# A decoder layer on one core: the cross-attention keys are split a stage earlier, and two orders of work are rewritten

## The reference, cut to what matters

```python
x = x + attention(layernorm(x), Wq, Wk, Wv, Wo)       # causal; 32 heads of 16 in 8 groups; batch 4, 512 tokens, width 512
x = x + cross(layernorm(x), ctx, ctx)                 # 8 heads; per batch q, k, v are (8, 64, 512) views of the 512 x 512 array
x = x + ffn(layernorm(x), w_gate, w_up, w_down)       # 2048 wide, quantised: weights to -1, 0, 1, activations to 8 bits
# cross, for each of the 4 x 8 heads (m, n over 512 columns, d over 64 rows):
qk = einsum('bdm,bdn->bmn', qh, kh) / 8
ret = einsum('bmn,bcn->bcm', softmax(qk, axis=-1), vh)
# quantised weight: clip(round(w / scale), -1, 1), scale = mean(|w|) + 1e-5
```

## Time and profile before

| | us |
|---|---|
| median of 3 runs (range) | 791.97 (790.47 to 792.49) |
| the profiled execution's own time | 791.34 |
| its span in the trace | 789.5 |
| busy: PE, DVE, ACT, POOL | 758.5, 637.8, 491.1, 423.1 |
| projections, to the first full step | about 0 to 98 |
| self-attention, to the barrier | about 98 to 373.9 |
| attention output | 373.9 to about 435 |
| cross-attention | about 435 to 595 |
| feed-forward | about 595 to 789 |

### The profile page before, as it was taken

How to read it: one execution, slowest core, us unless ns; L and a number is a source line. 1 busy time by engine, 2 the same in 40 slices (tenths; PEclk the granted TensorE clock), 3 DMA queues, 4 the chain that set the end, 5 groups by cost and what they waited for, 6 DMA issues and landing times.

```text
span 789.5 us, 15365 instructions
## 1 busy us (share of the span) xinstructions
PE 758.5 (96%) x4832; PEld 420.6 (53%) x4886; DVE 637.8 (81%) x1905; ACT 491.1 (62%) x844; POOL 423.1 (54%) x459
## 2 busy tenths in 40 slices
PE   8999999999999999998999899999998999999998
PEld 6777544444444444443777555555543455455543
DVE  7676888889888889881589878888977899888883
ACT  4665567667766776676355555555556576567564
POOL 5554489999999700000234367777886444423331
PEclk9999999999999999999899999999999999999999
DMA  8898674444544311200486434444420011000001
GB/s 289 301 385 282 210 186 136 122 132 133 139 128 130 96 54 52 61 18 3 146 284 236 162 108 136 134 136 135 121 70 18 11 42 41 28 15 27 28 26 42
DMA packets 65888, 94.79 MB, mean 120 GB/s; under 512 B 27184, under 2 KB 38576, under 8 KB 64272
## 3 DMA queue, kind: packets, MB, share of 16 engines
q1 hardware_dynamic: 61344, 80.77, 32.5%
q0 software_dynamic: 3952, 12.98, 5.8%
q10 hardware_dynamic: 512, 0.07, 0.1%
HBM read 72.88 MB, written 20.51 MB: 118 GB/s over the span
## 4 chain that ended last, share of the span: by engine, by line
PE 40%; DVE 5%; issue 3%; ACT 2%; POOL 1%; SPq 0%; DMA 0%; ACTq 0%; DVEq 0%; POOLq 0%
PE r_p L1698 12%; PE r_p L1633 7%; PE r_pn L1646 7%; PE r_p L1728 3%; PE r_pn L1728 3%; PE r_p L1605 3%; PE r_p L1661 2%; PE r_p L1712 2%; DVE r_stats L1384 1%; DVE tok L1403 1%; PE r_p L1587 1%; DVE r_xl L1397 1%; ACT r_xn L1235 1%; DVE r_mx L1416 0%; DVE r_h L1500 0%
## 5 line engine op out<-in xcount | busy, mean ns | idle before, releaser
L787 ACT ACTIVATE b_probs<-ab_j 128x512 f32<-128x512 f32 (+1 forms) x352 | 176.7, 560 | 25.5 <-PE ab_j L852 14.6
L148 DVE CUSTOM_DVE_ANT_0 b_junk<-ab_t,mask_qk 128x128 bf16<-128x128 f32 (+2 forms) x243 | 108.7, 485 | 27.0 <-PE ab_t L128 26.7
L852 PE MATMUL ab_j<-qs,ks 98*128 98x512 bf16 (+1 forms) x352 | 121.8, 361 | 2.9 <-DMA qs<-mrow 1.1
L1277 ACT ACTIVATE r_probs<-r_p 128x512 f32<-128x512 f32 x128 | 69.5, 599 | 65.2 <-PE r_p L1633 63.8
L148 DVE CUSTOM_DVE_ANT_0 b_junk<-ab_e,mask_qk 128x256 bf16<-128x256 f32 (+2 forms) x237 | 103.6, 482 | 0.3 <-issue 0.2
L1416 DVE TENSOR_REDUCE r_mx<-r_p 128x1 f32<-128x512 f32 x128 | 82.4, 675 | 22.1 <-PE r_p L1605 21.2
L1175 POOL TENSOR_TENSOR r_halves<-r_probs 128x1024 f32<-128x1024 f32 x32 | 76.6, 2395 | 34.8 <-DVE r_total L1446 24.9
L1327 ACT ACTIVATE r_silu<-r_p,r_cg 128x512 f32<-128x512 f32 x64 | 44.2, 691 | 53.0 <-PE r_p L1698 51.7
L870 PE MATMUL ab_pv<-b_probs,v 128*32 128x512 f32 (+3 forms) x1024 | 75.6, 436 | 0.0
L1202 POOL TENSOR_SCALAR r_h<-r_h,r_fh 128x1024 f32<-128x1024 f32 x32 | 38.0, 1199 | 64.8 <-DVE r_fh L1546 64.8
L128 PE MATMUL ab_e<-ks,qs 96*128 96x128 bf16 (+3 forms) x269 | 64.0, 300 | 5.3 <-DVE mx L148 0.7
(11 more groups left out here) (177 smaller groups left out, 1761.3 us busy)
## 6 DMA issues: line engine op xcount, KB each, us to landing
qs<-q_parts SPq DMA_DIRECT2D x32, 192.0 KB, 3.3
q_parts<-a_parts SPq DMA_DIRECT2D x15, 384.0 KB, 6.1
a_wst<-in_w_gate SPq DMA_DIRECT2D x4, 1024.0 KB, 7.7
a_wst<-in_w_up SPq DMA_DIRECT2D x4, 1024.0 KB, 9.9
a_wst<-in_w_down SPq DMA_DIRECT2D x4, 1024.0 KB, 8.3
qs<-q_parts SPq DMA_DIRECT2D x32, 128.0 KB, 3.2
b_wst<-in_w_gate POOLq DMA_DIRECT2D x16, 256.0 KB, 3.8
b_wst<-in_w_up POOLq DMA_DIRECT2D x16, 256.0 KB, 3.3
```

The costliest lines, as they stand in the source:

```text
L148: best = nc.vector.tensor_tensor_reduce(out=junk[:, 2 * (st.use[i, k] % slots) + n, 0:w], in0=bank[:, c:c + w], in1=keep["mask_qk"][:, SEQ ...
L787: nc.scalar.activation(pblock(j % 2, kb)[:, j0:j0 + nj, c:c + w], p2[(NE * j + n) % BANKS2][:, 0:nj * w].rearrange("p (j c) -> p j c", j=n ...
L852: last = nc.tensor.matmul(bank, ks[0:STACK + 2, s, kb * P:(kb + 1) * P], qs[0:STACK + 2, s, j0:j0 + nj, kb * P + c:kb * P + c + w], start= ...
L1277: nc.scalar.activation(probs[:, 2 * (p % 2) + a, blk, :], p2_bank("s", j, n)[:], ACT.Exp, scale=SCALE).then_inc(p2_used, 1)
```

## The change

Three things change.

1. The step of self-attention has another order on PE, on DVE (through `Steps.order`) and on ACT, where `osb` is kept after the ninth exponential instead of the fifth.
2. The split of the keys moves from cross-attention into self-attention's steps 21 to 36, one pair per step: GpSimd loads the raw rows after it has quantised all weights, ACT makes the high part at the end of its step, GpSimd subtracts and stores both parts to DRAM, and cross-attention's SP loads both. The pairs of steps 34, 35 and 36 follow on ACT straight after its last `osb`. GpSimd waits for the last stores before the barrier. With it the second of the three quantising instructions gets a second operation (subtract, min), and the third becomes max, min.
3. `sum_probs` works once for four heads, with weights of 32 columns; the totals have 8 slots, sums and reciprocals go by four heads, and the final multiplication of a pair moves from body 13 to body 17 behind its first. `D_LAST` grows by four, so twelve feed bodies lie beside `attend_context` instead of eight.

```diff
-        self.order = [0, 1, self.OUT, 2, self.TURN] + list(range(3, self.nu))
+        self.order = [0, 1, 2, self.TURN, 3, 4, 5, 6, 7, self.OUT, 8, 9]
...
+    KPAIRS, KEYS_FROM = BATCH * XHEADS // 2, LAST - BATCH * XHEADS // 2
+    key_raw = wst[:, 0:2, :]
+    key_h = nc.alloc_sbuf_tensor_at("b_key_h", [P, 2, DIM], F32R, offset=keep["wst_at"] + 2 * 4 * DIM)
+    key_l = nc.alloc_sbuf_tensor_at("b_key_l", [P, 2, DIM], F32R, offset=keep["wst_at"] + 4 * 4 * DIM)
+    PARTS = KD * FF // PART
+    key_in, key_high, key_low, key_out = wst_in[0:2], wq2, wq1, m.sems("key_out", 2)
+    LOADED, QUANTISED = 16 * PARTS, 3 * PARTS
...
-            nc.gpsimd.tensor_scalar(out, raw, MAGIC, None, ALU.subtract).then_inc(wq2, 1)
+            nc.gpsimd.tensor_scalar(out, raw, MAGIC, 1.0, ALU.subtract, ALU.min).then_inc(wq2, 1)
             pool.wait_ge(wq2, t + 1)
-            nc.gpsimd.tensor_scalar(out, out, 1.0, -1.0, ALU.min, ALU.max)
+            nc.gpsimd.tensor_scalar(out, out, -1.0, 1.0, ALU.max, ALU.min)
...
+        def load_keys(p):
+            if p >= KPAIRS:
+                return
+            if due(p - 1):
+                pool.wait_ge(key_low, QUANTISED + p - 1)
+            pool.dma_start(key_raw[:, p % 2, :], io["ctx"][P * p:P * (p + 1), :]).then_inc(key_in[p % 2], 16)
+
+        def split_keys(p):
+            pool.wait_ge(key_high, QUANTISED + p + 1)
+            if due(32 * (p // 2)):
+                pool.wait_ge(key_out[p % 2], 32 * (p // 2))
+            nc.gpsimd.tensor_tensor(key_l[:, p % 2, :], key_raw[:, p % 2, :], key_h[:, p % 2, :].bitcast(F32), ALU.subtract).then_inc(key_low, 1)
+            pool.wait_ge(key_low, QUANTISED + p + 1)
+            for name, tile in (("kh", key_h), ("kl", key_l)):
+                pool.dma_start(scr[name][P * p:P * (p + 1), :], tile[:, p % 2, :].bitcast(F32)).then_inc(key_out[p % 2], 16)
+
+        pool.wait_ge(wq2, QUANTISED)
+        load_keys(0)
+        load_keys(1)
+        for p in range(KPAIRS):
+            split_keys(p)
+            load_keys(p + 2)
+        for s in range(2):
+            pool.wait_ge(key_out[s], 32 * (KPAIRS // 2))
...
-            for n in range(5):
+            for n in range(9):
...
-            for n in range(5, NE):
+            for n in range(9, NE):
                 exponential(n)
+            p = i - KEYS_FROM
+            if 0 <= p < KPAIRS:
+                act.wait_ge(key_in[p % 2], LOADED + 16 * (p // 2 + 1))
+                if due(32 * (p // 2)):
+                    act.wait_ge(key_out[p % 2], 32 * (p // 2))
+                nc.scalar.activation(key_h[:, p % 2, :], key_raw[:, p % 2, :], ACT.Copy).then_inc(key_high, 1)
...
-            F(0); S(0); F(1); S(1)
+            F(0); F(1); S(0); F(2)
+            W(0); W(1); W(2); W(3)
+            turn_maxima(nc, pe, st, keep, i)
+            S(1); F(3); S(2); S(3); F(4); F(5); S(4); S(5); F(6); F(7); S(6); S(7)
             turn_outputs()
-            F(2); S(2)
-            turn_maxima(nc, pe, st, keep, i)
-            F(3); S(3)
-            F(4); S(4)
-            W(0); W(1); W(2); W(3)
-            F(5); S(5); F(6); S(6); F(7); S(7); F(8); S(8); F(9); S(9); S(10)
+            S(8); F(8); S(9); F(9); S(10)
...
+            def load_keys(p):
+                if p >= 2:
+                    sp.wait_ge(k_in[p % 2], 16 * (p // 2))
+                if due(STEP * 2 * (p - UNROLL + 1)):
+                    sp.wait_ge(scores, STEP * 2 * (p - UNROLL + 1))
+                sp.dma_start(kh[:, p % UNROLL, :].bitcast(F32), scr["kh"][P * p:P * (p + 1), :]).then_inc(k_in[p % 2], 16)
+
+            def load_keys_low(p):
+                if due(STEP * 2 * (p - 1)):
+                    sp.wait_ge(scores, STEP * 2 * (p - 1))
+                sp.dma_start(kl[:, p % 2, :].bitcast(F32), scr["kl"][P * p:P * (p + 1), :]).then_inc(kl_in[p % 2], 16)
...
-            def keys(p):
-                act.wait_ge(k_in[p % 2], 16 * (p // 2 + 1))
-                if due(STEP * 2 * (p - UNROLL + 1)):
-                    act.wait_ge(scores, STEP * 2 * (p - UNROLL + 1))
-                nc.scalar.activation(kh[:, p % UNROLL, :], k2[:, p % 2, :], ACT.Copy).then_inc(kh_done, 1)
...
-            def keys_low(p):
-                dve.wait_ge(kh_done, p + 1)
-                if due(STEP * 2 * (p - 1)):
-                    dve.wait_ge(scores, STEP * 2 * (p - 1))
-                nc.vector.tensor_tensor(kl[:, p % 2, :], k2[:, p % 2, :], kh[:, p % UNROLL, :].bitcast(F32), ALU.subtract).then_inc(kl_done, 1)
...
-            def sum_probs(p):
-                pe.wait_ge(first_total, p + 1)
-                pe.wait_ge(second_total, p + 1)
-                if p < LATE_SUMS:
-                    pe.wait_ge(p2_used, p2_use["sum", p] - SBANKS + 1)
-                elif p == LATE_SUMS:
+            def sum_probs(q):
+                pe.wait_ge(first_total, 2 * q + 2)
+                pe.wait_ge(second_total, 2 * q + 2)
+                if q < QUADS - 1:
+                    pe.wait_ge(p2_used, p2_use["sum", q] - SBANKS + 1)
+                else:
                     pe.wait_ge(p2_used, P2_USES)
-                else:
-                    pe.wait_ge(p2_used, p2_use["sum", p - 1] + 1)
-                for a in range(2):
-                    last = nc.tensor.matmul(p2_bank("sum", p)[a * H:(a + 1) * H, :], keep["ones64"][:], total[:, 2 * (p % 2) + a, :], start=True, stop=True)
+                for a in range(4):
+                    last = nc.tensor.matmul(p2_bank("sum", q)[a * PART:(a + 1) * PART, :], keep["ones64"][:, 0:PART], total[:, (4 * q + a) % TSLOTS, :],
+                                            start=True, stop=True)
                 last.then_inc(summed, 1)
...
-                p = pair_due(i, 8)
-                if p is not None and p < LATE_SUMS:
-                    sum_probs(p)
+                q = quad_due(i, 10)
+                if q is not None and q < QUADS - 1:
+                    sum_probs(q)
```

173 lines of the change are left out of this document (84 added, 89 removed).

## The result

The changed kernel takes 891.66 us (median of 4 runs, 890.50 to 892.78) against 791.22 (788.73 to 792.49) in the same comparison: 1.127 times as long, 95% interval 1.124 to 1.131. The forecast was 782. The profiled execution took 892.78 with a span of 891.0.

The account below looks back on a forecast made before the run. PE was taken to bound the kernel, busy 758.5 of 789.5 us. The terms: 791.3 - 11.7 + 10.5 - 1.8 - 6.9 = 781.4; with the median 0.6 above the profiled execution, 782 us, range 775 to 792.

Parts of the forecast that it names:

- The quantised weights must be ready earlier: GpSimd's quantising in self-attention: line 760 falls from 1485 ns to 0.65 us, 48 parts end 40 us earlier, near 232.
- 24 us are to spare: Self-attention keys: first raw keys land at 236, ACT asks near 260, so nothing waits.
- Quantising stays slow: Rival, 13 in 100: GpSimd's weights finish at 272, ACT waits for keys at step 21, +13, so 795 us.
- The new order: Self-attention steps: 0.40 us gained in 28 steps, 0.5 for draining steps, together -11.7 us.
- the two waits: PE's two short waits in a self-attention step, 0.40 us together with a small gap, bounded by 0.32 and 0.48.
- the order brings nothing: Rival, 10 in 100: a new wait in self-attention holds the step at 8.7 us, giving 793.
- DVE's loop of 8.3: Self-attention step: DVE's closed loop takes 8.3 us, barely below PE's own work of 8.35.
- The end of self-attention: Barrier after self-attention: the key transfers' uncovered tail starts the second block 10.5 us later, bounds 8 to 14.
- with 0.3 for the barrier 12.8: End of self-attention: last store lands 12.5 us after the last osb begins, barrier opens at 12.8.
- The clock: PE behind the self-attention barrier: already at 0.50 before the change, so the longer gap adds nothing to the sum.
- Attention output: ACT's two key copies and DVE's first subtraction leave this part: -1.8 us, range 0 to -2.5.
- The sums: Cross-attention: 16 sums at 0.90 become 8 at 0.94 for four heads each, -6.9 us.

Follow-up runs that it names:

- the fast pairs: Changed kernel with two GpSimd quantising operand pairs replaced: times 1.0 plus -MAGIC, and min then max; 790.26 us, ratio 0.999.
- the old pairs: Changed kernel with the kernel before's two GpSimd operand pairs (subtract alone; min then max); 806.83 us, ratio 1.019.
- e9: Kernel before with the new order of a step, except that TensorE turns the outputs where it did before; 778.80 us, ratio 0.986.
- the mended kernel: Changed kernel with faster GpSimd operand pairs and all sixteen key copies in self-attention steps 19 to 31; 766.10 us, ratio 0.969.
- e8: An experiment sharing the kernel before's order behind the barrier; the text does not say which one, so no time can be assigned.
- e7: Another experiment sharing the kernel before's order behind the barrier; the text does not say which one, so no time can be assigned.
- e4: Kernel before with only the changed kernel's order of a step in self-attention; 775.28 us, ratio 0.979.

## Why the prediction was wrong

The step that failed is **"The quantised weights must be ready earlier"**: "A `tensor_scalar` of two operations with the same types and shape, line 416, takes 621. The edit makes line 760 such an instruction. I take 0.65." It is not such an instruction. Line 416 multiplies and adds; line 769 subtracts and takes a minimum, and that pair takes 1.92. The duration was taken from an instruction that shared types, shape and number of operations, where what decides is which operations stand in which order. The row that warned was the earlier trace rows itself: one operation at 1485 ns beside two at 621 says that the count isn't what sets it.

- **The bounds of that step** were 0.62 and 1.485, both rows of other pairs. The real value lay above both. And the clamp, whose two operands the diff exchanges, was costed at nothing without a word, though its 0.61 us of the earlier trace rows was known for the other order alone: (1.92 - 0.61) x 48 = 63 us. (The 59 us of the same step, what key work beside PE would cost uncovered, count four issues for each pair, where there are three: 16 x (1.29 + 3 x 0.6) = 49. It entered no sum.)
- **"24 us are to spare"** held as arithmetic: with the fast pairs the last part starts at 230.3, the first key copy waits for nothing, and with the old pairs the stall is 18.1, where the rival had +13.
- **The rival "Quantising stays slow"** named the place, the waiting instruction and the mechanism, with 13 in 100, and its test: ACT waiting at the end of step 21. Its price stopped at the old duration. A rival in which an edit makes an instruction slower than it was would have given, at 5.26 us a part, 48 x 1.73 = 83 us on top of the 18 of stall with the old pairs.
- **The new order** was forecast at -11.7 and measured at -12.7 up to the barrier. The full steps gained 0.50, where the two waits read from the earlier trace rows gave 0.40, and the draining steps 2.9 where I had added 0.5, while the first `osb` copy came 4.2 later. The rival that the order brings nothing, and the worry that DVE's loop of 8.3 had no slack, are refuted: steps of 8.23 us show that the loop is shorter than that. That each of the two waits goes with one move, as I thought before e9, is refuted by it: the whole gain of a full step stays with the outputs turned early.
- **The end of self-attention** was forecast at +10.5, bounds 8 to 14, and measured at 22.16 - 2.34 = +19.8. The chain of GpSimd's transfers was right: last store issued 11.0 behind `osb` (forecast 9.9), landed by 13.9 (12.5). What failed is "with 0.3 for the barrier 12.8": the barrier also waits for GpSimd's drain, 8.0 us for its 97 transfers. No row that I had chosen showed it.
- **The clock** behind the barrier: after 21 us of idle PE ran at 0.50 for some 8 us (484.5 to 492.8), where the kernel before had 0.50 in the earlier trace rows. From the barrier to the end the changed kernel took 406.5 us and the mended one, at 1.00 there, 404.1; the kernel before took 415.6, and e8, with the same instructions behind the barrier and 1.00 there, 412.8. So the half clock costs 2.4 to 2.8 us whether the gap before it is short or long, and the sum was right to take nothing for the longer one. The Trainium skill ("TensorE: Matmul & The Clock Gate", Part 1) says that an idle array falls back to the low level; the 21 us here agree with it.
- **Attention output**, -1.8 forecast: -1.7, or -1.3 against e7 and e8, whose clock there is that of the mended kernel. **The sums**, -6.9 forecast: -6.3, by 16 x 0.90 - 8 x 1.00 = 6.4. Four matmuls side by side cost 1.00, the product with v having said 0.94. The Trainium skill's speedup for three column tiles ("TensorE: Matmul & The Clock Gate", Part 3) would have given an estimated 1.18; the measured 1.00 lies nearer to the row of the product. The rest, 1.2, lies in the start of the feed-forward part, where I had nothing.

The sum with the measured terms: 791.3 - 12.7 + 101.3 + 19.8 - 1.7 - 6.3 - 1.2 = 890.5, where the profiled execution took 892.8. Of the 2.3 left over 2.2 are ahead of the barrier, by comparison with e4: the first `osb` copy comes 0.6 later, the 28 steps take 1.1 more than the stall, most of it right behind the stall at half clock, and the draining steps with their key copies 0.5. The key copies don't lengthen the full steps: from step 3 to step 31 it is 230.9 us with the fast pairs and 231.0 in e4, which has no key work there.

Without the two pairs the change would have been a draw (790.3), and not the 782 of the forecast, since the drain took the rest. The order, the sums and the attention output are all worth what they were meant to be worth, which the 766 us of the mended kernel show.

## What to carry to other kernels

A duration is carried over from another row only if the operations and their order are the same, not just types, shape and count. If a diff exchanges two operands, that edit has a price to be looked up, and when no row has it, the upper bound lies above every row at hand, not at the old value. Before a wait is added to an engine that has run free, ask by how much its new supplier may be late and multiply that by the number of its parts: 1.73 us a part times 48 made 83 us of this loss, and the 18 that the old pairs were late the rest. At a barrier that follows an engine's last transfers, leave room for its drain, or do the transfers so early that the drain is hidden.

## What the hardware showed that I had not expected

- GpSimd's `tensor_scalar` on 128x512 takes 0.61 us for times-add, add-times and min-max, 1.49 for a single operation and 1.92 for every other pair tried (fp32 or bf16 in, bf16 out).
- GpSimd's DRAIN at a block's end takes about 0.04 us and 0.082 for each transfer it issued since its last drain (0.12 to 0.13 for one, 4.07 for 49, 7.99 for 97), loads and stores alike, and waits for those still under way. A drain placed in an idle stretch takes that part out of the next one.
- Behind the barrier PE's granted clock isn't the same in all executions with the old order: 0.54 over 374 to 378 us in the kernel before, 1.00 in two of the experiments that share its order there (e7 and e8). What decides between them stays open. It is worth about 2.8 us (415.6 from the barrier to the end against 412.8).
